# Three PSUM banks in a fixed order for the ten projections of an attention step, and a copy of v moved ahead of part of the gate weights' split

## The chip, the cores and the metric

One core of one Trainium2 chip runs the whole program in a single launch. The metric is the device time of a run in microseconds (us). The engines are TensorE (PE in the profile, with its weight loads as PEld), VectorE (DVE), ScalarE (ACT), GpSimd (POOL) and SyncE (SP), whose queue issues the DMAs.

## The reference

A block of linear attention with decay, and after it a dense layer with a mixture of low-rank experts, both with a layer norm in front and a residual. Cut to what matters:

```
q = rope(x @ Wq.T); k = rope(x @ Wk.T); v = x @ Wv.T      # 32 heads of q, 8 of k and v, 128 wide
dt = softplus(x @ Win.T + dt_bias); g = -dt * exp(A_log_bias)
per chunk of 128 tokens, G = cumsum(g):
  y  = (q k^T * exp(G_i - G_j), causal) @ (v dt)  +  (q exp(G)) @ state
  state = state * exp(G_last) + (k exp(G_last - G))^T @ (v dt)
y = y / rms(y) * gnorm_w * silu(x @ Wg.T)
x = x + y @ Wo.T
x = x + dense(norm(x)) + experts(norm(x))
```

x is 4 images of 512 tokens by 512 features, all in fp32. To keep precision, each fp32 product is taken as three products of "high" and "low" parts in the format fp32r: hi x hi, lo x hi and hi x lo. So every weight and every operand is split into a high half (a copy by ScalarE) and a low half (a subtraction by VectorE).

## The kernel before

Three stages follow each other. The first norms and transposes x, makes the tables, and computes the projections of the first step. The second, attention, has 32 steps, n = 0 to 31. A step takes one group g of heads (8 groups: one head of k and v, four of q) and one image b (4), n = 4 g + b. In the text, "the first step of a group" has b = 0 and "the last step" b = 3. The third stage is the output projection, the second norm and the experts.

TensorE's code is written out for all 32 steps. The other engines run group 0, then a hardware loop over groups 1 to 6, then group 7.

In each step TensorE makes ten projections (units 0 to 9): for the step itself the four gates G0 to G3, one for each chunk of 128 tokens, and for the next step K, Q0 to Q3 and V. Each is 12 matmuls of 128x512 (4 pieces of the contraction, 3 products each). The order on TensorE in a step is: scores of chunk 0, K (unit 0), the state's matmul of chunk 0, G0 (1), mix of chunk 0; scores 1, Q0 (2), state 1, G1 (3), mix 1; scores 2, Q1 (4), state 2, G2 (5), mix 2; Q2 (6), scores 3, Q3 (7), G3 (8), transposes of k, V (9), mix 3, transposes of v.

Each projection fills one PSUM bank. Before the change there are two, and unit number modulo 2 says which. So a unit may start when the unit two before it has been read out (`bank_free`): K and the Qs are read by VectorE, which rotates them (`rotate`, L99: three products, L103 to L105, the last of which counts `rope_terms`); the gates by ScalarE (tanh) and VectorE (`make_gate`, L768, which counts `gate_set`); V by ScalarE (`save_v_rows`, L933, tile `v_t`, which counts `v_set`). GpSimd adds the two rope products (`add_rope`, L108, which counts `roped`).

All engines take their instructions in order, so the order written by hand in `step` matters. On ScalarE the end of a step is: tanh of G3, `save_k`, the high half 1 of wg, `q_high` of the next step's chunk 0 (which waits until all five rope sums of the next step are made), `save_v_rows`, the high half 2 of wg, `save_v` (the copy of the transposed v, tile `v_tok`). The halves of wg occur only in the last step of a group. On VectorE the end of the same step is: gate 3, the low half 1 of wg, `q_low` of the next step's chunk 0, the low half 2 of wg. VectorE splits the low halves of the next wq (L747) near the start of a group's last step, ahead of K's rotation, and ScalarE and VectorE those of wkv in between.

SyncE's queue loads, in one order, the rows of g (`g_row`, 256 KB, one load a chunk), of e, stores z, and in a group's first step loads the next wkv (512 KB, at chunk 1) and wq (2 x 512 KB, at chunk 2), in its last step wg (2 x 512 KB). The row load at chunk 3 is that of the next step's chunk 1; GpSimd waits for its landing (`row_landed(n + 1, 1)`) between its adds for Q2 and Q3.

Of the kernel before, what the change touches and what calls it, by code (L numbers as in the profile page):

```python
# [32 lines left out]
B, L, HID = 4, 512, 512  # L33
# [5 lines left out]
NC = L // C  # L39
# [6 lines left out]
UNITS = 10  # L46
ROPED = 1 + HG
# [5 lines left out]
def wait_ge(engine, sem, count):  # L53

    if not isinstance(count, int) or count > 0:
        engine.wait_ge(sem, count)


def part(w_raw, i):

    return w_raw[i][:, :].rearrange("p (k n) -> p k n", k=KT if i == 0 else KT // 2)


def dst(w, i):

    return w[:, :, :] if i == 0 else w[:, (i - 1) * 2:i * 2, :]
# [354 lines left out]
def attention_stage(nc, io, keep):  # L421
    shared, tab, ident, g_dram, e_dram, z_dram = (keep[k] for k in ("shared", "tab", "ident", "g_dram", "e_dram", "z_dram"))
    with ExitStack() as ctx:
# [3 lines left out]
        def pb(name):  # L427
            return ctx.enter_context(nc.psum_tensor(name, [P, HG, P], F32))

        def sem(name):  # L430
            return ctx.enter_context(nc.semaphore(name))

        w_raw, wkv, wq, wg = (keep[k] for k in ("w_raw", "wkv", "wq", "wg"))
# [23 lines left out]

        z_st = sb("z_st", [P, 2, TB, HG, NC // 2, BL])

        p_proj = [pb(f"p_proj{i}") for i in range(2)]  # L460
        p_y = [pb(f"p_y{i}") for i in range(2)]
        p_score, p_cst = (pb(n) for n in ("p_score", "p_cst"))
        p_tok = keep["p_tok"]
# [5 lines left out]
        rope_terms, roped, v_set = keep["rope_terms"], keep["roped"], keep["v_set"]  # L469
# [4 lines left out]
        gate_set, tanh_set, decay_set = sem("gate_set"), sem("tanh_set"), sem("decay_set")  # L474
        k_split, v_split, q_split, g_split = sem("k_split"), sem("v_split"), sem("q_split"), sem("g_split")
        wk_hi, wv_hi, wq_hi, wg_hi = sem("wk_hi"), sem("wv_hi"), sem("wq_hi"), sem("wg_hi")
# [7 lines left out]
        K_UNIT, V_UNIT, Q_UNIT, GATE_UNIT = 0, 9, (2, 4, 6, 7), (1, 3, 5, 8)  # L484
        LAST = B * KVH - 1

        def ahead(n):

            return not (isinstance(n, int) and n == LAST)
# [3 lines left out]
            return UNITS * n + (at if ahead(n) else GATE_UNIT.index(at))  # L493

        def bank(n, b, at):
            return p_proj[(at if ahead(n) else GATE_UNIT.index(at)) % 2]

        def steps(engine, first, step):

# [10 lines left out]
        def has_last(n):  # L510

            return not (isinstance(n, int) and n == 0)
# [4 lines left out]
        def group_ahead(g):  # L517
            return not (isinstance(g, int) and g == KVH - 1)
# [80 lines left out]

        @block.tensor  # L600
        def _(pe):
            def bank_free(n, b, at):

                if not ahead(n):
                    i = GATE_UNIT.index(at)
                    if i >= 2:
                        pe.wait_ge(gate_set, NC * n + i - 1)
                    elif i == 1:
                        pe.wait_ge(v_set, n + 1)
                    else:  # L610
                        pe.wait_ge(gate_set, NC * n)
                elif at == 0:
                    wait_ge(pe, gate_set, NC * n)
                elif at == 1:
                    pe.wait_ge(v_set, n + 1)
                elif at - 2 in GATE_UNIT:
                    pe.wait_ge(gate_set, NC * n + GATE_UNIT.index(at - 2) + 1)
                else:
                    r = 0 if at - 2 == K_UNIT else 1 + Q_UNIT.index(at - 2)
                    pe.wait_ge(rope_terms, ROPED * (n + 1) + r + 1)  # L620

            def gates(g, b, n, c):
                bank_free(n, b, GATE_UNIT[c])
# [112 lines left out]
        def _(dve):  # L736
# [13 lines left out]
            def g_low_weights(g, i):  # L750

                dve.wait_ge(wg_hi, 2 * g - 2 + i)
                dve.tensor_tensor(dst(wg[1], i), part(w_raw, i), dst(wg[0], i).bitcast(F32), ALU.subtract).then_inc(g_split, 1)
# [21 lines left out]
            def make_probs(n, c):  # L775
                m = NC * n + c
                dve.wait_ge(score_done, m + 1)
                dve.wait_ge(decay_set, m + 1)
                dve.tensor_tensor(probs[:, c % 2], p_score[:, :, :], probs[:, c % 2], ALU.mult).then_inc(probs_set, 1)  # L779
# [52 lines left out]
            def opening_lows(n, pieces):  # L832
                if not ahead(n):
                    for k in pieces:
                        opening_low(dve, keep, k)

            def step(g, b, n):
                make_probs(n, 0)
                q_low(n, b, 1)
                if has_last(n):  # L840
                    make_z(n - 1, 3)
                if group_ahead(g) and b == B - 1:
                    q_low_weights(g + 1)
                if has_last(n):
                    turn_z(n - 1, 3)
                opening_lows(n, (0, 1))
                rotate_next(g, b, n, K_UNIT, 0)
                make_state(n, b, 0)
                make_gate(g, b, n, 0)
                if group_ahead(g) and b == B - 2:  # L850
                    kv_low(wk_hi, k_split, g + 1, 0)
                for c in (1, 2):
                    make_probs(n, c)
                    scale_q(g, b, n, c)
                    q_low(n, b, c + 1)
                    make_z(n, c - 1)
                    opening_lows(n, (2 * c, 2 * c + 1))
                    rotate_next(g, b, n, Q_UNIT[c - 1], c)
                    turn_z(n, c - 1)
                    make_state(n, b, c)  # L860
                    make_gate(g, b, n, c)
                    if c == 1 and group_ahead(g) and b == B - 1:
                        kv_low(wv_hi, v_split, g + 1, D)
                rotate_next(g, b, n, Q_UNIT[2], 3)
                make_probs(n, 3)
                scale_q(g, b, n, 3)
                make_z(n, 2)
                opening_lows(n, (6, 7))
                rotate_next(g, b, n, Q_UNIT[3], 4)
                turn_z(n, 2)  # L870
                if ahead(n):
                    k_low(n + 1, b + 1)
                make_gate(g, b, n, 3)
                if group_ahead(g) and b == B - 1:
                    g_low_weights(g + 1, 1)
                if ahead(n):
                    q_low(n + 1, b + 1, 0)
                if group_ahead(g) and b == B - 1:
                    g_low_weights(g + 1, 2)

            steps(dve, first, step)
            make_z(LAST, 3)
            turn_z(LAST, 3)

        @block.scalar
        def _(act):
# [5 lines left out]
            def half_high(w, i, done, loads):  # L892

                act.wait_ge(w_in[i], 16 * loads)
                act.activation(dst(w[0], i), part(w_raw, i), ACT.Copy).then_inc(done, 1)
# [47 lines left out]
            def save_v(n):  # L943
                act.wait_ge(tok_done, 2 * n + 2)
                wait_ge(act, xw_set, 3 * n)
                wait_ge(act, y_done, NC * n)
                act.activation(v_tok[:, :, :], p_tok[:, :, :], ACT.Copy).then_inc(tok_saved, 1)  # L947
# [13 lines left out]
            def step(g, b, n):  # L961
                if has_last(n):
                    squares(n - 1, 3)
                q_high(n, b, 1)
                make_decay(n, b, 1)
                make_tanh(g, b, n, 0)
                if group_ahead(g) and b == B - 2:
                    act.wait_ge(unit_done, unit(n, K_UNIT) + 1)
                    kv_high(wk_hi, g + 1, 0)
                if not ahead(n):  # L970
                    act.wait_ge(keep["gn_in"], 16)
                opening_highs(n, (0, 1))
                for c in (1, 2):
                    squares(n, c - 1)
                    q_high(n, b, c + 1)
                    make_decay(n, b, c + 1)
                    if c == 1 and group_ahead(g) and b == B - 1:
                        kv_high(wv_hi, g + 1, D)
                    make_tanh(g, b, n, c)
                    opening_highs(n, (2 * c, 2 * c + 1))  # L980
                squares(n, 2)
                if ahead(n):
                    k_high(n + 1, b + 1)
                    make_decay(n + 1, b + 1, 0)
                make_tanh(g, b, n, 3)
                if ahead(n):
                    save_k(n + 1)
                    if group_ahead(g) and b == B - 1:
                        half_high(wg, 1, wg_hi, 2 * g + 2)
                    q_high(n + 1, b + 1, 0)  # L990
                    save_v_rows(n, b)
                    if group_ahead(g) and b == B - 1:
                        half_high(wg, 2, wg_hi, 2 * g + 2)
                    save_v(n + 1)
                    if group_ahead(g) and b == B - 2:
                        act.wait_ge(unit_done, unit(n, Q_UNIT[3]) + 1)
                        half_high(wq, 1, wq_hi, 2 * g + 1)
                        half_high(wq, 2, wq_hi, 2 * g + 1)
                opening_highs(n, (6, 7))
# [588 lines left out]
```

## Time and profile before

| | |
|---|---|
| median of 3 runs | 1941.15 us (1938.84 to 1943.4) |
| the profiled execution | 1941.0 us, span 1939.2 us |
| mean granted TensorE clock | 0.983 of full |
| TensorE matmuls busy | 1832.8 us, 95% of the span |
| VectorE | 1270.4 us, 66% |
| ScalarE | 693.4 us, 36% |
| GpSimd | 643.0 us, 33% |
| DMA | 173.54 MB, 89 GB/s over the span |
| attention stage | from about 77 to 1430 us |

The span runs from the first to the last instruction. Busy time is the time in which an engine works on an instruction; idle time is put down to what ended it ("the releaser"). The granted clock is the share of 2.4 GHz that TensorE was allowed: 1.00 is the level of 2.4 GHz, 0.5 that of 1.2 GHz, and a value between them is a mean over a stretch that has both.

### The profile page before, as it was taken

How to read it: one execution, taken by the hardware profiler on the slowest of the kernel's cores; microseconds unless marked ns; L12 is line 12 of the kernel's file. 1: busy time of each engine (PE TensorE's matmuls, PEld its weight loads, DVE VectorE, ACT ScalarE, POOL GpSimd, SP SyncE). 2: the span in 40 equal slices, each digit the busy share in tenths (PEclk: the TensorE clock that was granted, in tenths of full speed). 3: DMA queues.
4: the chain of work that ended last, by engine and by line, in shares of the span. 5: the costliest groups of instructions: out<-in, count | busy, mean ns of one | idle time of the engine just before them, and what ended most of it. 6: DMA issues, size and time to landing. Idle time of an engine off the chain costs nothing. (4 is left out here: it accounts for less than half of the span.)

```text
span 1939.2 us, 27787 instructions
## 1 busy us (share of the span) xinstructions
PE 1832.8 (95%) x8856; PEld 1482.9 (76%) x8856; DVE 1270.4 (66%) x2340; ACT 693.4 (36%) x2186; POOL 643.0 (33%) x741
## 2 busy tenths in 40 slices
PE   6799999999999999999999999999887999999997
PEld 5588777777777777777777778777766888888885
DVE  7777777787777777777777777777764333333332
ACT  4533443343344434334444434343443112112111
POOL 3444444444444444443444444344400010110100
PEclk9899999999999999999999999999988999999998
DMA  4132332223232223323322232322454322323321
GB/s 153 50 99 83 91 93 70 67 98 92 82 90 94 71 66 93 95 83 91 93 63 70 87 104 77 94 64 63 135 174 155 99 83 81 98 81 92 98 76 33
DMA packets 111073, 173.54 MB, mean 89 GB/s; under 512 B 8016, under 2 KB 45904, under 8 KB 110928
## 3 DMA queue, kind: packets, MB, share of 16 engines
q1 hardware_dynamic: 110928, 171.80, 29.6%
q8 instruction: 67, 1.10, 0.2%
q14 instruction: 78, 0.64, 0.1%
HBM read 133.50 MB, written 38.27 MB: 89 GB/s over the span
## 5 line engine op out<-in xcount | busy, mean ns | idle before, releaser
L84 PE MATMUL p_proj<-wg_hi,shared 128*128 128x512 f32 x1024 | 362.8, 435 | 0.0
L84 PE MATMUL p_proj<-shared,wq_hi 128*128 128x512 f32 x992 | 340.5, 405 | 20.3 <-DVE rope_b L105 20.3
L113 POOL TENSOR_TENSOR q<-rope_a,rope_b 128x512 f32<-128x512 f32 x128 | 165.8, 1295 | 348.8 <-DVE rope_b L105 248.8
L84 PEld LDWEIGHTS p_proj<-wg_hi,shared 128*128 128x128 f32 x1024 | 194.2, 190 | 85.5 <-issue 46.5
L911 ACT ACTIVATE tanh<-p_proj 128x512 f32<-128x512 f32 x128 | 76.6, 599 | 488.5 <-PE p_proj L84 488.5
L84 PEld LDWEIGHTS p_proj<-shared,wq_hi 128*128 128x128 f32 x992 | 189.5, 191 | 69.4 <-DVE rope_b L105 25.5
L84 PE MATMUL p_proj<-wg_lo,shared 128*128 128x512 f32 x512 | 203.3, 397 | 0.0
L84 PE MATMUL p_proj<-shared,wq_lo 128*128 128x512 f32 x496 | 198.6, 400 | 0.0
L84 PE MATMUL p_proj<-shared,wkv_hi 128*128 128x512 f32 x496 | 169.4, 402 | 18.3 <-DVE rope_b L105 18.3
L687 PE MATMUL p_y<-v_tok,probs 128*128 128x128 f32 x1024 | 182.1, 275 | 0.0
L904 ACT ACTIVATE probs<-g_row,stab 128x128 f32<-128x128 f32 x512 | 164.6, 406 | 33.2 <-POOL g_row L1018 33.2
L103 DVE TENSOR_TENSOR rope_a<-p_proj,cos 128x512 f32<-128x512 f32 x155 | 105.0, 677 | 103.0 <-PE p_proj L84 103.0
L929 ACT ACTIVATE square<-p_y 128x128 f32<-128x128 f32 x512 | 134.7, 280 | 91.6 <-PE p_y L687 80.3
L821 DVE SCALAR_TENSOR_TENSOR z<-p_y,srstd,gate 128x128 f32<-128x128 f32 x512 | 143.7, 342 | 29.2 <-issue 19.4
L1144 DVE TENSOR_TENSOR wq_lo<-w_raw,wq_hi 128x1024 fp32r<-128x1024 f32 x63 | 77.1, 1224 | 128.8 <-ACT wq_hi L1139 128.8
L779 DVE TENSOR_TENSOR probs<-p_score,probs 128x512 f32<-128x512 f32 x128 | 88.3, 690 | 97.9 <-PE p_score L84 83.7
L687 PEld LDWEIGHTS p_y<-v_tok,probs 128*128 128x128 f32 x1024 | 150.1, 192 | 3.0
L1036 POOL TENSOR_TENSOR srstd<-svar,mhalf 128x4 f32<-128x4 f32 x128 | 147.6, 1153 | 10.0
L686 PE MATMUL p_y<-state,qs 128*128 128x128 f32 x768 | 148.1, 274 | 0.0
L1488 POOL TENSOR_TENSOR var<-mv,eps 128x1 f32<-128x1 f32 x16 | 3.1, 192 | 432.0 <-DVE mv L1407 432.0
L1028 POOL TENSOR_TENSOR xw<-v_tok,stab 128x512 f32<-128x512 f32 x96 | 104.4, 1088 | 104.7 <-ACT v_tok L947 104.7
L686 PEld LDWEIGHTS p_y<-state,qs 128*128 128x128 f32 x768 | 123.5, 191 | 8.8
(181 smaller groups left out, 3711.3 us busy)
## 6 DMA issues: line engine op xcount, KB each, us to landing
g_row<-g_scratch SPq DMA_DIRECT2D x128, 256.0 KB, 6.0
z_scratch<-z_st SPq DMA_DIRECT2D x256, 128.0 KB
w_raw<-z_scratch SPq DMA_DIRECT2D x63, 512.0 KB, 5.9
e_row<-e_scratch SPq DMA_DIRECT2D x96, 256.0 KB, 3.9
w_raw<-in_wq_t SPq DMA_DIRECT2D x16, 512.0 KB, 8.2
w_raw<-in_wg_t SPq DMA_DIRECT2D x16, 512.0 KB, 5.6
w_raw<-in_wo_t SPq DMA_DIRECT2D x11, 512.0 KB, 5.8
w_raw<-in_wkv_t SPq DMA_DIRECT2D x8, 512.0 KB, 5.0
```

What stands on the lines that cost most here:

```text
L84: mm = pe.matmul(out, lhs[a], rhs[e], start=(i == 0 and j == 0), stop=(i == len(pairs) - 1 and j == 2))
L103: dve.tensor_tensor(rope_a[:, s, :], x, keep["cos"][:, :], ALU.mult)
L113: pool.tensor_tensor(out, keep["rope_a"][:, s, :], keep["rope_b"][:, s, :], ALU.add).then_inc(keep["roped"], 1)
L686: pe.matmul(p_y[c % 2][:, h, :], qs[:, h, :], state[:, c % 2, h, :], start=True, stop=False)
L687: mm = pe.matmul(p_y[c % 2][:, h, :], probs[:, c % 2, h, :], v_tok[:, c, :], start=(c == 0), stop=True)
L779: dve.tensor_tensor(probs[:, c % 2], p_score[:, :, :], probs[:, c % 2], ALU.mult).then_inc(probs_set, 1)
L821: zz = dve.scalar_tensor_tensor(z[:, h, :], p_y[c % 2][:, h, :], srstd[:, c, h:h + 1], gate[:, c % 2, h * D:(h + 1) * D], ALU.mult, ALU.mult)
L904: e = act.activation(probs[:, c % 2, h, :], g_row[:, c % 2, h, :], ACT.Exp, bias=stab[:, b % 2, c, T_BIAS, h:h + 1])
L929: s = act.activation(square[:, h, :], p_y[c % 2][:, h, :], ACT.Square, scale=2.0 / float(np.sqrt(D)), accum_out=ssum[:, c, h:h + 1])
L1028: pool.tensor_tensor(xw[:, c % 2], v, w, ALU.mult).then_inc(xw_set, 1)
L1036: pool.tensor_tensor(srstd[:, c, :], svar[:, c, :], mhalf[:, :], ALU.pow).then_inc(srstd_set, 1)
L1144: dve.tensor_tensor(by_half(keep["z_lo"][slot]), raw_z(keep, raw_slot), by_half(keep["z_hi"][slot].bitcast(F32)), ALU.subtract).then_inc(k ...
```

## The change

The attention stage gets a third bank, and a table says which bank a unit takes. Before a unit starts, TensorE waits until the last unit in the same bank has been read out, in the same step or in the step before. The last step of all, which makes only the four gates, has a table of its own. So K follows Q3 of the step before, G0 follows V, Q0 follows G3 of the step before, G1 follows G0, Q1 follows K, G2 follows Q0, Q2 follows G1, Q3 follows Q1, G3 follows G2, and V follows Q2. In a group's last step, ScalarE makes both high halves of wg later (order: `q_high`, `save_v_rows`, half 1, `save_v`, half 2), and VectorE both low halves after `q_low`.

```diff
-        p_proj = [pb(f"p_proj{i}") for i in range(2)]
+        p_proj = [pb(f"p_proj{i}") for i in range(3)]
...
+        BANKS = (0, 1, 2, 1, 0, 2, 1, 0, 2, 1)
+        LAST_BANKS = (0, 1, 2, 0)
...
         def bank(n, b, at):
-            return p_proj[(at if ahead(n) else GATE_UNIT.index(at)) % 2]
+            return p_proj[BANKS[at] if ahead(n) else LAST_BANKS[GATE_UNIT.index(at)]]
...
+            def taken(n, at):
+
+                if at in GATE_UNIT:
+                    wait_ge(pe, gate_set, NC * n + GATE_UNIT.index(at) + 1)
+                elif at == V_UNIT:
+                    pe.wait_ge(v_set, n + 2)
+                else:
+                    r = 0 if at == K_UNIT else 1 + Q_UNIT.index(at)
+                    pe.wait_ge(rope_terms, ROPED * (n + 1) + r + 1)
+
             def bank_free(n, b, at):
 
                 if not ahead(n):
                     i = GATE_UNIT.index(at)
-                    if i >= 2:
-                        pe.wait_ge(gate_set, NC * n + i - 1)
-                    elif i == 1:
-                        pe.wait_ge(v_set, n + 1)
-                    else:
-                        pe.wait_ge(gate_set, NC * n)
-                elif at == 0:
-                    wait_ge(pe, gate_set, NC * n)
-                elif at == 1:
-                    pe.wait_ge(v_set, n + 1)
-                elif at - 2 in GATE_UNIT:
-                    pe.wait_ge(gate_set, NC * n + GATE_UNIT.index(at - 2) + 1)
-                else:
-                    r = 0 if at - 2 == K_UNIT else 1 + Q_UNIT.index(at - 2)
-                    pe.wait_ge(rope_terms, ROPED * (n + 1) + r + 1)
+                    if LAST_BANKS[i] in LAST_BANKS[:i]:
+                        return taken(n, GATE_UNIT[LAST_BANKS.index(LAST_BANKS[i])])
+                    return taken(n - 1, max(u for u in range(UNITS) if BANKS[u] == LAST_BANKS[i]))
+                here = [u for u in range(at) if BANKS[u] == BANKS[at]]
+                if here:
+                    return taken(n, here[-1])
+                if has_last(n):
+                    taken(n - 1, max(u for u in range(UNITS) if BANKS[u] == BANKS[at]))
...
                 make_gate(g, b, n, 3)
-                if group_ahead(g) and b == B - 1:
-                    g_low_weights(g + 1, 1)
                 if ahead(n):
                     q_low(n + 1, b + 1, 0)
                 if group_ahead(g) and b == B - 1:
+                    g_low_weights(g + 1, 1)
                     g_low_weights(g + 1, 2)
...
                     save_k(n + 1)
-                    if group_ahead(g) and b == B - 1:
-                        half_high(wg, 1, wg_hi, 2 * g + 2)
                     q_high(n + 1, b + 1, 0)
                     save_v_rows(n, b)
                     if group_ahead(g) and b == B - 1:
+                        half_high(wg, 1, wg_hi, 2 * g + 2)
+                    save_v(n + 1)
+                    if group_ahead(g) and b == B - 1:
                         half_high(wg, 2, wg_hi, 2 * g + 2)
-                    save_v(n + 1)
```

## Rows read from the trace of the kernel before

**Rows 1.** The page's first part: busy us, share, instructions by engine.

```profile
PE 1832.8 (95%) x8856; PEld 1482.9 (76%) x8856; DVE 1270.4 (66%) x2340; ACT 693.4 (36%) x2186; POOL 643.0 (33%) x741
```

**Rows 2.** TensorE's groups (busy, mean ns, idle before) and one of its waits (us, times, longest).

```profile
L84 PE MATMUL p_proj<-shared,wq_hi 128*128 128x512 f32 x992 | 340.5, 405 | 20.3 <-DVE rope_b L105 20.3
L84 PE MATMUL p_proj<-shared,wkv_hi 128*128 128x512 f32 x496 | 169.4, 402 | 18.3 <-DVE rope_b L105 18.3
...
PE p_tok L655 <- ACT v_t L936: 4.3, 5, 1.5
```

**Rows 3.** Timeline around V of step 13, TensorE and ScalarE: start, us, instruction, [idle before].

```profile
661.44 0.49 PE L648 MATMUL p_tok<-ident,k 128*128 128x128 f32 x3
662.54 0.50 PE L84 MATMUL p_proj<-shared,wkv_hi 128*128 128x512 f32 x1 [0.61 <-DVE rope_b L105]
...
667.22 0.60 PE L655 MATMUL p_tok<-ident,v_t 128*128 128x128 f32 x4
667.58 0.47 PE L84 MATMUL p_score<-q_hi,k_hi 128*128 128x512 f32 x1
...
703.75 0.50 PE L84 MATMUL p_proj<-shared,wkv_hi 128*128 128x512 f32 x1 [0.61 <-DVE rope_b L105]
...
665.64 0.60 ACT L936 ACTIVATE v_t<-p_proj 128x512 f32<-128x512 f32 x1 [1.11 <-PE p_proj L84]
```

**Rows 4.** TensorE's timeline in step 15, a group's last step: scores 0, K, scores 1, Q0.

```profile
708.79 0.47 PE L84 MATMUL p_score<-q_hi,k_hi 128*128 128x512 f32 x1
...
709.57 0.40 PE L84 MATMUL p_proj<-shared,wkv_hi 128*128 128x512 f32 x1
...
712.36 1.02 PE L672 MATMUL p_cst<-xw,k_tok 128*128 128x512 f32 x2
...
716.82 0.47 PE L84 MATMUL p_score<-q_hi,k_hi 128*128 128x512 f32 x1
...
720.12 0.50 PE L84 MATMUL p_proj<-shared,wq_hi 128*128 128x512 f32 x1 [2.36 <-DVE rope_b L105]
...
724.56 1.02 PE L672 MATMUL p_cst<-xw,k_tok 128*128 128x512 f32 x2
```

**Rows 5.** VectorE's timeline in step 15: wq's low halves, K's rotation, state, Q2's rotation.

```profile
715.11 2.35 DVE L747 TENSOR_TENSOR wq_lo<-w_raw,wq_hi 128x1024 fp32r<-128x1024 f32 x2
...
720.10 0.69 DVE L808 COPY state<-p_cst 128x512 f32<-128x512 f32 x1
...
742.03 0.69 DVE L103 TENSOR_TENSOR rope_a<-p_proj,cos 128x512 f32<-128x512 f32 x1 [3.36 <-PE p_proj L84]
```

**Rows 6.** Timeline of step 16, a group's first: SyncE's issue, GpSimd, TensorE; the issues' landing.

```profile
785.91 1.24 SPq L536 DMA_DIRECT2D g_row<-g_scratch  x2
...
794.77 1.26 POOL L113 TENSOR_TENSOR q<-rope_a,rope_b 128x512 f32<-128x512 f32 x1 [7.08 <-DMA g_row<-g_scratch]
...
797.24 0.66 PE L655 MATMUL p_tok<-ident,v_t 128*128 128x128 f32 x4 [1.05 <-ACT v_t L936]
...
DMA to landing us min/median/max: 8.5/8.6/8.7
```

**Rows 7.** ScalarE's wg copies as a group; timeline of step 16, ScalarE's squares, VectorE's probs.

```profile
L895 ACT ACTIVATE wg_hi<-w_raw 128x1024 fp32r<-128x1024 f32 x14 | 14.8, 1059 | 0.0
...
757.24 0.28 ACT L929 ACTIVATE square<-p_y 128x128 f32<-128x128 f32 x1 [2.17 <-issue]
...
756.89 0.69 DVE L779 TENSOR_TENSOR probs<-p_score,probs 128x512 f32<-128x512 f32 x1 [1.85 <-issue]
...
773.10 0.69 DVE L779 TENSOR_TENSOR probs<-p_score,probs 128x512 f32<-128x512 f32 x1 [0.19 <-PE p_score L84]
```

**Rows 8.** Stretches: busy (x) by engine, granted clock, DMA share, GB/s.

```profile
65.00:80.00 15.00, 7.29 (x24) 5.17 (x25) 8.75 (x18) 8.02 (x18) 4.61 (x6) 0.54 0.37 87
212.70:217.10 4.40, 4.34 (x17) 3.23 (x18) 3.37 (x7) 1.81 (x5) 4.17 (x5) 1.00 0.41 133
720.10:724.50 4.40, 4.38 (x12) 3.47 (x13) 4.00 (x9) 1.81 (x5) 4.28 (x5) 0.61 0.40 130
```

## The prediction

> **What bounds the kernel now.** I began at the page's busy times [rows 1]: TensorE is busy for 1832.8 of 1939.2 us and no other engine for more than 66%. Inside the attention stage nothing but TensorE's own stream can set the time, and a change that takes no matmul away can only return idle time of that engine. So the second view was TensorE's idle time by what ended it [rows 2]. The rope products on VectorE end 18.3 us of idle time ahead of V's projections and 20.3 us ahead of Q projections; the copy of v ends 4.3 us ahead of the transposes of v. Listing the waits one by one (TensorE's timeline, in pieces, over the whole stage) gave three kinds: 31 waits ahead of V, one in every step but the last, of 0.52 us in steps 0 to 3 and 28 to 30 and 0.61 us in the other 24; seven ahead of Q0, of 2.34 to 2.36 us, in step 3 of each group but the last; five of 0.69 to 0.92 us ahead of Q0 in the first step of groups 2 to 6. 7 x 2.35 + 3.87 = 20.3, so the list is whole.
>
> **V's wait, and its price.** The middle of a step without loads [rows 3]: three transposes of k start at 661.44, V at 662.54, 1.10 us later. Four transposes of v take 0.36 us from start to the scores' start (667.22 to 667.58), so three should take 0.27: V starts 0.83 us later than it need, not the 0.61 that the idle column shows, because the refill of the pipeline is lost too. (For the 0.52 waits: 0.74.) With two banks V takes the bank of Q3, whose rotation VectorE has just ended. With the new table V takes bank 1, last used by Q2, which VectorE rotates before probs, qs and z of chunk 3 and before Q3, some 5 us earlier. Gone: 24 x 0.83 + 7 x 0.74 = 25.1 us.
>
> Does something else stop TensorE there? Behind V stand the last mix and the transposes of v, which need ScalarE's copy v_t. In this step ScalarE stood idle for 1.11 us until V was done, and v_t ended at 666.24, 0.98 us ahead of the transposes [rows 3]. V comes 0.83 earlier, so the copy still follows V at once (0.28 left), and the transposes have all of their 0.98. In ordinary steps (41.2 us from one V to the next, 662.54 to 703.75) the 0.83 is kept.
>
> **Q0's wait in a group's last step.** VectorE splits the next wq there: 2.35 us put ahead of K's rotation, which is over just before the state copy starts at 720.10 [rows 5]. Q0 stands in K's bank, so it starts at 720.12 where, counted as scores to projection in the same step (708.79 to 709.57, 0.78), it could have started at 716.82 + 0.78 = 717.60: 2.52 us [rows 4]. In the new table Q0 takes bank 2, freed by the previous step's last gate. A projection takes 2.79 (709.57 to 712.36), so the state matmul of chunk 1 is reached at 720.39; it needs the state that VectorE copies until 720.79, behind the same rotation. About 0.44 of the wait moves there, 2.08 is returned. VectorE then has no pause until it waits 3.36 us for Q2 [rows 5], more than the 2.08, so it has the slack. 7 x 2.08 = 14.6 us. The five waits in first steps give 3.87 + 5 x 0.17 = 4.7 (again the refill; the state copy is early enough by 0.2 to 0.5 us).
>
> **Where it is given back.** In a group's first step the weights of wkv and wq are loaded, 1.5 MB in the same queue. The g rows for the next step, issued at 785.91 behind them, let GpSimd go on at 794.77, after 7.08 us of waiting [rows 6]. GpSimd is in order: its add for Q3 stands behind that landing, ScalarE's q_hi behind the add, v_t behind q_hi, and the transposes of v behind v_t: 1.05 us of TensorE idle already in step 16, 0 to 1.47 in the seven first steps, and in the two without a wait (steps 0 and 12) v_t ends less than 0.1 us ahead of them. The issue hangs on the chunk-2 state of that step, so the landing does not move when only V moves: the whole of V's gain comes back as wait. 0.74 in step 0, 0.83 in step 4.
>
> In steps 8, 12, 16, 20 and 24 more comes back. VectorE there trails TensorE: probs of chunk 2 waited only 0.19 us for its scores [rows 7]. Its start is set by the loop's turn: the squares waited 2.17 us and probs 1.85 us on "issue" [rows 7], released by no semaphore. The change moves one wg_hi copy (1.06 us [rows 7]) behind v_tok, last before that turn. With v_tok 0.83 us earlier, the squares come 0.12 us later than now if the turn counts from the last copy's end; if the turn is hidden behind that copy, the low half of wg on VectorE, which now also ends later, still leaves K's rotation only 0.30 us earlier. I take the middle, 0.09 earlier, and with the 0.17 us of idle the whole chain to the landing moves 0.26 (0.05 to 0.47) instead of the 0.83 + 0.94 + 0.83 that TensorE has gained since the previous V: 2.34 us come back as wait, 11.7 in all. Given back: 0.7 + 0.8 + 11.7 = 13.3 us.
>
> The Trainium skill, "Runtime: NRT & Kernel Launch", section "Instruction fetch mechanics", says that a taken branch to a target that is not in the fetch window stalls until it is fetched. The two idle times on "issue" agree that the loop's turn stalls; whether a running copy hides it no row shows. By the rule, counted from the branch, it would be the 0.30 end, and the sum 1 us larger.
>
> **The moved operations otherwise.** The v_t copy now passes one wg_hi copy, but ScalarE was waiting for GpSimd there anyway (q_hi came late, v_t later still), so this buys nothing. The second low half on VectorE is needed only in the middle of G0 of the next step, at about 758.8 in the frame of step 16 against 756.5 when it is ready: 2.3 us of cover. No DMA moves in its queue; the wait of the loads of wg and wq on the splits is long met. One more bank costs nothing. The last step's gates wait for gates and rotations that are over.
>
> **The clock.** Of the seven long waits, the last four are followed by half clock: the granted clock reads 1.00 in the 4.4 us after the wait in groups 0 to 2 (212.7 is the first) and 0.61 in groups 3 to 6 (720.1 is the first) [rows 8], and Q0 takes 4.44 us instead of 2.82 [rows 4]: 1.6 us each, 6.4 in all. They go with the waits. But the wait ahead of v's transposes grows to about 2.5 to 4 us in five steps, as long as those or longer. At four in seven, five of them cost 5 x 4/7 x 1.6 = 4.6. Net +1.8.
>
> **The sum.** 25.1 + 14.6 + 4.7 = 44.4 returned, 13.3 given back, +1.8 of clock: 32.9 us. The profiled execution took 1941.0 us, of which 1939.2 are the span; the median shown is 1941.15, the same within 0.01%. 1941.0 - 32.9 = 1908.1: **1908 us**. Own range: the clock's part lies between +6.4 and -1.6, the loop's turn within 1 us, and a step's 0.98 us of slack may be shaved once g rows in last steps are the later ones: 1900 to 1915.
>
> **Rivals.**
> - *The landing moves too.* If the g rows arrive earlier than their issue suggests (it takes 8.6 us in first steps under the weight loads, so it may be the transfer that is slow and not the issue that is late), the 13.3 us are kept and no new half clock comes: 44.4 + 6.4 = 50.8, 1890 us. Against it: the queue is in order and the loads stand ahead. 0.12.
> - *The chain Q3, GpSimd, ScalarE, v_t sets every step.* If it is longer than I read by more than 0.28 + 0.98 = 1.26 us, V's gain comes back in ordinary steps too. Left: 14.6 and part of the clock, 1920 to 1928, say 1925. Against it are the 1.11 us of idle time in [rows 3]. 0.12.
> - *No change.* TensorE's wait was a mere label and the start of V or Q0 is set by something else, or VectorE's delay catches TensorE later in the same step: 1941. Against it: rope_b's end and V's start differ by 0.06 us or so at each of the waits I read. 0.05.
> - *Slower: the clock.* As the stage opens, after waits of 6.2, 1.6 and 2.5 us, TensorE works at half clock for about 14 us (0.54 over 65 to 80 us) [rows 8]. If each of the seven first steps' new waits did that, 7 x 7 = 49 us would be lost against 31.1 + 6.4 gained: 1953. It decides from a low stretch of 2 x 37.5/7 = 10.7 us per group. Against it: after 2.36 us the low stretch lasted about 3.4 us (1.6 lost). 0.03. The Trainium skill, "TensorE: Matmul & The Clock Gate", section "HAM oscillation", says that gaps in TensorE's work bring half clock for what follows each of them; the trace agrees in four cases of seven, and that page's rule speaks for this rival.
>
> **How the numbers follow.** My forecast has 0.68. The range 1896 to 1926 takes in my own range and the second rival, and leaves out the first, the third and the fourth (0.20). A change under 0.2% (3.9 us) is no change for this kernel. Faster 0.91, same 0.05, slower 0.04.
>
> **What would show it.** Right: no TensorE idle on rope_b; V follows k's transposes within 0.3 us; ordinary steps of 40.4 us; idle ahead of v's transposes grown from 4.3 to about 18 us, all in first steps, 2.5 to 4 us each from step 8 on; a new wait of 0.4 us on the state copy in last steps; a group of four steps from 170.2 to about 166.2 us plus half clock. Wrong: v's transposes wait in ordinary steps (second rival); their wait stays near 4 us (first rival); the mean granted clock falls below 0.983; VectorE has no idle time left ahead of Q2.

## The result, and the profile after

Four runs of the changed kernel took 1907.9 us (median; 1901.77 to 1910.72), beside 1942.27 us for the kernel before on the same chip: a ratio of 0.9822, 95% interval [0.9807, 0.9836]. Forecast were 1908 us, with a range of 1896 to 1926. The profiled execution took 1906.53 us, of which 1904.7 are the span, so 34.5 us less than the one of before; predicted were 32.9. Line numbers of the attention stage are four to seven higher than before.

The page's busy times, then three of its groups (busy, mean ns, idle before), for the changed kernel; they answer to [rows 1, 2]:

```profile
PE 1824.3 (96%) x8856; PEld 1481.1 (78%) x8856; DVE 1272.7 (67%) x2340; ACT 692.1 (36%) x2186; POOL 645.5 (34%) x741
...
L84 PE MATMUL p_proj<-shared,wq_hi 128*128 128x512 f32 x992 | 335.3, 399 | 0.0
...
L84 PE MATMUL p_proj<-shared,wkv_hi 128*128 128x512 f32 x496 | 171.4, 407 | 0.0
...
L935 ACT ACTIVATE square<-p_y 128x128 f32<-128x128 f32 x512 | 134.2, 279 | 85.7 <-PE p_y L694 80.4 <-issue 5.3
```

TensorE's waits of the same execution (us in total, times, longest):

```profile
PE p_tok L662 <- ACT v_t L942: 14.6, 9, 2.3
...
PE p_cst L679 <- DVE state L815: 5.3, 8, 3.3
```

All 38.6 us of idle time on `rope_b` are gone. What has come in their place is idle time ahead of v's transposes, grown from 4.3 to 14.6 us, and seven waits of 0.3 us on the state copy (the eighth, 3.3 us, is in step 31, stood there before too, and was not part of the sum).

TensorE's timeline of the changed kernel. First V in step 16, 0.25 us behind the transposes of k, then the state's matmul in step 15, then v's transposes in first steps 4 to 24 and in last step 19:

```profile
772.82 0.49 PE L655 MATMUL p_tok<-ident,k 128*128 128x128 f32 x3
773.07 0.48 PE L84 MATMUL p_proj<-shared,wkv_hi 128*128 128x512 f32 x1
...
708.71 1.10 PE L679 MATMUL p_cst<-xw,k_tok 128*128 128x512 f32 x2 [0.30 <-DVE state L815]
...
282.36 0.66 PE L662 MATMUL p_tok<-ident,v_t 128*128 128x128 f32 x4 [1.66 <-ACT v_t L942]
447.12 0.83 PE L662 MATMUL p_tok<-ident,v_t 128*128 128x128 f32 x4 [2.13 <-ACT v_t L942]
613.92 0.66 PE L662 MATMUL p_tok<-ident,v_t 128*128 128x128 f32 x4 [2.30 <-ACT v_t L942]
779.79 0.66 PE L662 MATMUL p_tok<-ident,v_t 128*128 128x128 f32 x4 [1.90 <-ACT v_t L942]
902.88 0.66 PE L662 MATMUL p_tok<-ident,v_t 128*128 128x128 f32 x4 [1.26 <-ACT v_t L942]
945.80 1.12 PE L662 MATMUL p_tok<-ident,v_t 128*128 128x128 f32 x4 [2.16 <-ACT v_t L942]
1112.32 0.66 PE L662 MATMUL p_tok<-ident,v_t 128*128 128x128 f32 x4 [2.27 <-ACT v_t L942]
```

The 4.4 us behind three of these waits (stretch, TensorE's busy time, granted clock, DMA share, GB/s). The stretch behind the 1.90 us stays at 2.4 GHz; 0.61 is a mean over a stretch that is mostly at 1.2 GHz:

```profile
447.10:451.50 4.40, 4.38 (x14) 0.61 0.00 0
613.90:618.30 4.40, 4.38 (x15) 0.61 0.00 0
779.80:784.20 4.40, 4.40 (x20) 1.00 0.00 0
```

**Where the time came from.** The start of k's transposes gives the length of each step. An interval runs from k's transposes near the end of one step to those of the next, so the V that it holds, and the wait of v's transposes, belong to the step before the one that fills most of it. The differences of the two profiled executions, with the prediction's terms sorted the same way:

| intervals from one step's k transposes to the next | before, us | after, us | saved | predicted |
|---|---|---|---|---|
| 7 over a group's last step (Q0's wait, V's wait, old half clock) | 313.0 | 286.6 | 26.4 | 26.7 |
| 7 ordinary | 288.4 | 282.4 | 6.1 | 5.7 |
| the last 3 (steps 28 to 30) | 123.5 | 121.1 | 2.4 | 2.3 |
| 5 pairs around the first steps 8, 12, 16, 20, 24 | 421.8 | 425.1 | -3.4 | -3.3 |
| the pair around step 4 | 83.37 | 82.79 | 0.58 | 0.74 |
| the first two (V of step 0, and its return as wait) | 80.12 | 79.85 | 0.27 | 0 |
| all of the span that lies outside (V of step 30) | 629.0 | 626.9 | 2.1 | 0.7 |

Intervals over last steps fell from between 43.8 and 45.4 us to 40.94 each, ordinary ones from 41.2 to 40.34. What the last row has above V's 0.7 us is at the end of the attention stage, where TensorE was at 1.2 GHz for 6.8 us from 1400 us on in the kernel before, and for 3.4 us near the same place after.

### The profile page after: what moved, and what is told of

It reads as the page before. It is cut to its first block and busy times, and to the rows that moved or that the text cites. A ratio compares the mean times of both kernels' runs of the same rounds, so it can differ in the third digit from the quotient of the medians.

```text
span 1904.7 us, 27787 instructions
## 1 busy us (share of the span) xinstructions
PE 1824.3 (96%) x8856; PEld 1481.1 (78%) x8856; DVE 1272.7 (67%) x2340; ACT 692.1 (36%) x2186; POOL 645.5 (34%) x741
## 5 line engine op out<-in xcount | busy, mean ns | idle before, releaser
L84 PE MATMUL p_proj<-shared,wq_hi 128*128 128x512 f32 x992 | 335.3, 399 | 0.0
L808 DVE TENSOR_TENSOR q_lo<-q,q_hi 128x512 fp32r<-128x512 f32 x128 | 91.6, 716 | 67.3 <-ACT q_hi L924 67.3
```

The lines of the kernel that those rows point to most:

```text
L84: mm = pe.matmul(out, lhs[a], rhs[e], start=(i == 0 and j == 0), stop=(i == len(pairs) - 1 and j == 2))
L808: dve.tensor_tensor(q_part[1][:, :, :], q[b % 2][:, :, c * C:(c + 1) * C], q_part[0][:, :, :].bitcast(F32), ALU.subtract).then_inc(q_lo_se ...
```

## The experiments

Letters stand for the kernels. Each ratio is against the kernel before, run beside it on the same chip. A, B, D and F shared a chip, C, E, G and H a second, I to L a third; times from different chips are compared by these ratios too.

**A. The change again.** No edit.

> The change itself, unaltered, as the neighbour of the other runs on this chip. Both theories: 1902 to 1911 us, 0.979 to 0.985 of before.

1907.7 us, ratio 0.9825 [0.9808, 0.9843]. The profiled execution is the slowest of its five, 1912.08 us, with 18.6 us ahead of v's transposes, where the first profile had 14.6. How long these waits are differs between executions of one kernel.

**B. The banks alone.** ScalarE and VectorE keep the old order of the wg halves.

```diff
+                if group_ahead(g) and b == B - 1:
+                    g_low_weights(g + 1, 1)
                 if ahead(n):
                     q_low(n + 1, b + 1, 0)
                 if group_ahead(g) and b == B - 1:
-                    g_low_weights(g + 1, 1)
                     g_low_weights(g + 1, 2)
```

and the same on ScalarE: both `half_high(wg, ...)` ahead of `save_v`, the first ahead of `q_high`.

> Three banks, with the old order of the gate weights' halves on ScalarE and VectorE. My theory: the banks make the whole gain, and the moved halves only delay VectorE's restart of the loop (its last low half ends about 1.4 us later in the frame of step 16), so K's rotation and, behind it, the g rows' issue in the five first steps inside the loop come up to 1.3 us earlier here: 0 to 6 us faster than the change, about 1904. Rival: the copy of v's rows ahead of the high half is worth something once V comes earlier (v_t would stand behind a copy of 1.06 us in seven steps): up to 7 us slower than the change, and the transposes of v then wait for v_t in every last step of a group.

1903.99 us, ratio 0.9811 [0.9785, 0.9838]. The banks carry the whole gain.

**C. The order alone.** The new order with the two old banks.

> Two banks as before, only the order of wg's halves on ScalarE and VectorE as in the change. My theory: nothing waits for the copy of v earlier, but VectorE's last low half ends later ahead of the loop's turn and K's rotation comes up to 1.3 us later in five first steps, where Q0 waits for it with two banks: 0 to 7 us slower than before, 1941 to 1948. Rival: the order is worth something by itself: faster than 1938.

1946.48 us, ratio 1.0025 [1.0013, 1.0037]: slower by a quarter of a per cent. Ahead of projections (first row), and Q0 in step 16 (second), with Q0's five waits in first steps now 1.10 to 1.89 us where the kernel before had 0.69 to 0.92:

```profile
PE p_proj L84 <- DVE rope_b L105: 42.6, 43, 2.4
...
766.16 0.50 PE L84 MATMUL p_proj<-shared,wq_hi 128*128 128x512 f32 x1 [1.88 <-DVE rope_b L105]
```

Both low halves of wg now stand behind `q_low` on VectorE, and wait there for ScalarE's high halves, so K's rotation comes later: in the mean of first steps 8 to 24 it starts 14.6 us after the k transposes of the step before, against 13.8 us in the kernel before. With two banks Q0 waits for just that rotation. With three it does not.

**D. wq's loads behind the rows, in the changed kernel.** The prediction put all that is given back on the g rows' landing behind wq's 1 MB. This moves the loads past the row load of chunk 3 and takes nothing out.

```diff
-                        if b == 0 and c == 2:
+                        if b == 0 and c == 3:
```

> The change, and in a group's first step the loads of wq are issued after the load of the g rows for the next step, not ahead of it. My theory: the transposes of v wait in first steps (12.9 of 14.6 us) because the g rows stand behind 1 MB of weights. They then land some 3 us earlier, those waits fall below 2 us in all, the four half clock stretches behind them go: 13 + 6 = 19 us faster than the change, about 1889. Rival: the wait is set by VectorE, which trails in these steps, or by the rows' late issue, not by the loads: waits of 10 us or more stay and the time stays above 1902.

1887.65 us, ratio 0.9726 [0.9708, 0.9744], 20 us below the change. SyncE's queue and GpSimd in step 16, first the changed kernel, then D:

```profile
767.89 0.98 SPq L534 DMA_DIRECT2D w_raw<-in_wq_t  x2
769.05 1.11 SPq L540 DMA_DIRECT2D g_row<-g_scratch  x2
...
777.33 1.26 POOL L113 TENSOR_TENSOR q<-rope_a,rope_b 128x512 f32<-128x512 f32 x1 [7.04 <-DMA g_row<-g_scratch]
```

```profile
758.02 0.39 SPq L540 DMA_DIRECT2D g_row<-g_scratch  x1
758.68 0.96 SPq L534 DMA_DIRECT2D w_raw<-in_wq_t  x2
759.93 0.34 SPq L540 DMA_DIRECT2D g_row<-g_scratch  x1
...
764.76 1.78 POOL L113 TENSOR_TENSOR q<-rope_a,rope_b 128x512 f32<-128x512 f32 x1 [4.27 <-DMA g_row<-g_scratch]
```

The rows that Q3's add waits for are issued ahead of the loads and are there 6.7 us later (758.02 to 764.76), against 8.3 us behind them (769.05 to 777.33). In the mean of first steps 8 to 24 they are issued 1.4 us earlier after the k transposes of the step before (36.0 against 37.5 us) and take 1.1 us less to land (7.1 against 8.2 us). v's transposes wait three times, 1.22 us at most, and no first step has half clock behind it.

**E. The same move in the kernel before.**

> The kernel before, and in first steps the loads of wq behind the g rows. My theory: it takes away only the 4.3 us of waits ahead of v's transposes, 1937; the 19 us that the same edit gave on top of the change are there only because the change moves TensorE ahead of the landing. Rival: the landing costs as much with two banks: 1922 to 1928.

1936.35 us, ratio 0.9973 [0.9961, 0.9984]. Its waits on `rope_b` stay whole:

```profile
PE p_proj L84 <- DVE rope_b L105: 38.6, 43, 2.4
```

So the same edit is worth 5 us to the kernel before and 20 us to the changed one. The difference, 15 us, is what the landing took back of the change's gain, half clock behind the waits included.

**F. V again behind Q3.** V's term alone is taken out.

```diff
-        BANKS = (0, 1, 2, 1, 0, 2, 1, 0, 2, 1)
+        BANKS = (0, 1, 2, 1, 0, 2, 1, 0, 2, 0)
```

> The change with one entry of the table altered: V takes bank 0, so it waits for Q3's rotation again (and K for the copy of V). Measures V's term alone. My theory: 0.83 us comes back in 19 of the 31 steps, 16 us slower than the change, less what shorter waits of v's transposes save of half clock (0 to 6): 1917 to 1924. Rival (V's label was empty): within 3 us of the change.

1919.9 us, ratio 0.9891 [0.9871, 0.9911]. V's 31 waits are back in their old size, and v's transposes wait less:

```profile
PE p_proj L84 <- DVE rope_b L105: 18.8, 31, 1.0
...
PE p_tok L662 <- ACT v_t L942: 8.7, 6, 3.0
```

V's part of the change is worth 12 us net, of 25.1 expected back from the waits alone.

**G. Q0 again behind K.** Q0's two terms are taken out, V's stays.

```diff
-        BANKS = (0, 1, 2, 1, 0, 2, 1, 0, 2, 1)
+        BANKS = (0, 1, 0, 1, 2, 0, 1, 2, 0, 1)
```

> The change with a table in which Q0 takes K's bank (0, 1, 0, 1, 2, 0, 1, 2, 0, 1), so it waits for K's rotation and nothing else gets tighter. Measures Q0's term alone. My theory: the seven waits of 2.35 us are back (14.6 us net) and half clock with some of them (0 to 7 x 1.6), the five of first steps cost nothing because they only shorten the wait of v's transposes, which saves half clock there (up to 6): 1918 to 1930, most likely 1924. Rival: Q0's wait only hid VectorE's delay and TensorE meets it later in the step: within 3 us of the change.

1930.22 us (1925.83 to 1934.8), ratio 0.9941 [0.9916, 0.9965], at the top of what was expected. Q0 in two last steps, 3 and 15, and in two first steps, 16 and 20, then the sum:

```profile
210.53 0.50 PE L84 MATMUL p_proj<-shared,wq_hi 128*128 128x512 f32 x1 [2.34 <-DVE rope_b L105]
...
713.00 0.80 PE L84 MATMUL p_proj<-shared,wq_hi 128*128 128x512 f32 x1 [2.33 <-DVE rope_b L105]
756.21 0.50 PE L84 MATMUL p_proj<-shared,wq_hi 128*128 128x512 f32 x1 [1.16 <-DVE rope_b L105]
...
923.45 0.50 PE L84 MATMUL p_proj<-shared,wq_hi 128*128 128x512 f32 x1 [1.88 <-DVE rope_b L105]
...
PE p_proj L84 <- DVE rope_b L105: 23.5, 12, 2.3
```

As in C, Q0's waits in first steps are longer than in the kernel before, by the new order. Q0's part is worth 22.5 us (1930.2 less 1907.7, and the same by the two ratios), with the new order in place; the profiled execution of G has seven stretches at 1.2 GHz in the stage, where the change had four.

**H. B and D together.** The banks alone, with wq's loads behind the rows.

> Three banks, the old order of wg's halves, and the loads of wq behind the g rows. My theory: with no wait left that hangs on VectorE's restart, the old order is worth nothing more: within 2 us of the change with the loads moved, 1885 to 1888. Rival: the old order's 4 us are kept, about 1883, or v_t stands behind the first high half in last steps and it is 3 us slower, 1891.

1889.63 us, ratio 0.9728 [0.9706, 0.9749], no different from D (0.9726), though 1.6 us above what was expected. It has 4.2 us of idle time ahead of v's transposes, in last steps. In two of them (steps 3 and 7) the old order on VectorE meets GpSimd's add for Q3, which takes 2.3 us there. First H in step 7 (VectorE, GpSimd), then the changed kernel in the same step:

```profile
400.72 1.22 DVE L760 TENSOR_TENSOR wg_lo<-w_raw,wg_hi 128x1024 fp32r<-128x1024 f32 x1
...
400.73 2.33 POOL L113 TENSOR_TENSOR q<-rope_a,rope_b 128x512 f32<-128x512 f32 x1 [5.43 <-DMA g_row<-g_scratch]
```

```profile
401.80 1.27 POOL L113 TENSOR_TENSOR q<-rope_a,rope_b 128x512 f32<-128x512 f32 x1 [5.19 <-DMA g_row<-g_scratch]
```

**I. VectorE's new order, ScalarE's old one, with D's edit.**

```diff
                     save_k(n + 1)
+                    if group_ahead(g) and b == B - 1:
+                        half_high(wg, 1, wg_hi, 2 * g + 2)
                     q_high(n + 1, b + 1, 0)
                     save_v_rows(n, b)
                     if group_ahead(g) and b == B - 1:
-                        half_high(wg, 1, wg_hi, 2 * g + 2)
-                    save_v(n + 1)
-                    if group_ahead(g) and b == B - 1:
                         half_high(wg, 2, wg_hi, 2 * g + 2)
+                    save_v(n + 1)
```

> ScalarE splits both halves of the gate weights' high part ahead of v_tok, as in the kernel before; VectorE keeps the new order (one low half, then the probabilities, then the other low half), and wq's loads are issued after the rows. Theory: in last steps GpSimd's add for Q3 is stretched by VectorE's two-input work beside it (1.63 us in the change, 2.33 us with the banks alone), and with the new order on VectorE alone it stays at 1.6 us or below, so the order of ScalarE is worth nothing: 1887 us, within 3 us of the changed kernel with wq after the rows (1887.65). Rival: the copy of v needs its early place on ScalarE, since v_tok starts 1 us later behind the second high half and v's transposes wait for it: 1892 us or above, with v's transposes idle in the last steps by 1 us or more each.

1886.34 us (1885.57 to 1887.23), ratio 0.9718 [0.9697, 0.9739]. Ahead of v's transposes 0.5 us are left in the whole kernel:

```profile
PE p_tok L662 <- ACT v_t L942: 0.5, 2, 0.3
```

The early copy of v is worth nothing here. GpSimd's longest add for Q3 in a last step is 1.77 us, not "1.6 or below", so that part of the expectation was off.

**J. The same without D's edit.**

> The changed kernel with ScalarE's order put back to both high halves ahead of v_tok, VectorE's new order kept, wq's loads where they are. Theory: the waits of v's transposes in the first steps stay at 1.7 to 2.3 us each from step 4 on, and those of the last steps go away or stay under 0.5 us: 1904 us, inside 1899 to 1908. Rival, ScalarE's early copy carries part of the gain: 1910 us or above, with waits of 1 us and more at v's transposes in the last steps.

1899.62 us (1897.12 to 1906.87), ratio 0.9797 [0.9773, 0.9822]; the last steps' waits did not go away (0.97 us in step 3, 1.05 in step 19), and those of first steps from step 4 on were 0.83 to 2.36 us, where 1.7 to 2.3 each was expected; 12.1 us in all.

**K and L. The banks alone, and the change, on the chip of I and J.**

> The banks alone once more, beside the whole change on the same chip. If the copy's new place is worth nothing, the ratio is 0.981 again and no more than 0.1% from the change's. If it is worth what the stretched add on GpSimd costs (0.7 us in each of seven last steps, 5 us), it comes 3 to 5 us above the change, a ratio near 0.985. If it costs, as the first call's 1904 against 1907.7 suggests, it comes 3 to 4 us below.

> The changed kernel as it is, for the comparison on the same chip with the three others: 1908 us, a ratio of 0.982, as in both calls before.

K: 1902.61 us, ratio 0.9808 [0.9782, 0.9834]. L: 1905.5 us, ratio 0.9835 [0.9808, 0.9862]. The change's median lies 3.7 us above that of the banks alone in the first pair and 2.9 us above in the second, with intervals that overlap both times. So the new order bought nothing, and may cost some 4 us. J, which has only VectorE's half of it, lies 5.9 us below L; their intervals overlap a little.

The traces show how ScalarE's half can cost. VectorE's low halves need ScalarE's high halves of the same weights. In the changed kernel ScalarE makes them late and VectorE waits for each; in J it waits for neither. Step 15, first the changed kernel, then J:

```profile
738.13 1.23 DVE L760 TENSOR_TENSOR wg_lo<-w_raw,wg_hi 128x1024 fp32r<-128x1024 f32 x1 [0.74 <-ACT wg_hi L901]
739.57 1.77 DVE L760 TENSOR_TENSOR wg_lo<-w_raw,wg_hi 128x1024 fp32r<-128x1024 f32 x1 [0.21 <-ACT wg_hi L901]
```

```profile
735.27 2.35 DVE L760 TENSOR_TENSOR wg_lo<-w_raw,wg_hi 128x1024 fp32r<-128x1024 f32 x2
```

In the mean of first steps 8 to 24, counted from the k transposes of the step before, K's rotation then starts at 14.6, 14.3 and 14.0 us in the three profiles of the change, at 13.6 and 13.3 with the banks alone and at 13.2 in J; the g rows are issued at 37.5, 37.5 and 37.2, at 37.1 and 36.9, and at 36.4 us. The order of these kernels is that of their times. That the whole 5.9 us come from there is not shown, and in D against I (1887.65, 1886.34), with the first steps' waits gone, there is no difference.

## Why the prediction was right

**What bounds the kernel, and V's wait.** Held. No idle time on `rope_b` is left, V follows k's transposes in 0.25 us, and an ordinary step takes 40.34 us where 40.4 was written: 0.87 us less each, 0.83 predicted. V's price had to be read from start to start; the idle column alone (0.61) adds up to 18.3 us over the stage, almost 7 too few. The copy v_t did keep its slack in ordinary steps: v's transposes wait in none of them, which ends the rival of the chain through Q3, GpSimd and ScalarE. In last steps that chain does come through at times (0.44 us in step 11, 1.26 in step 19, 1.9 us over four of them), which the prediction had only as a remark in its range.

**Q0's wait.** Held: 26.4 us over the last steps against 26.7 (14.6 of Q0, 5.7 of V, 6.4 of half clock). The wait that moves to the state copy is 0.28 to 0.30 us, not 0.44. G gives the same part the other way round. It costs 22.5 us to take back Q0's part, against 14.6 + 4.7 returned and up to 6.4 of clock. C and G also show a cover that the prediction did not price: the new order makes Q0's waits in first steps 0.2 to 1.2 us longer, and only the third bank hides that.

**Where it is given back.** The mechanism is right, by D and E: with the rows ahead of wq's loads the change keeps 15 us more than the kernel before gains by the same edit. The mis-sized term is the 2.34 us that come back in each of five first steps. Measured from k's transposes of the step before, GpSimd goes on after the landing 45.8 us later in the mean of the five, against 46.4 before: the chain moved 0.58 us, where 0.26 was chosen and 0.47 was the upper bound. The issue is not what moved (37.5 against 37.4 us); the landing came 0.7 us sooner after it. "The landing does not move" was taken from the issue alone. Without half clock the five pairs saved 3.0 us (6.4 less 3.4), not 1.3. In steps 0 and 4 together 0.1 us more was kept than predicted.

The sign written down for this part came out only in kind. Idle time ahead of v's transposes was to be about 18 us, all in first steps, 2.5 to 4 us each from step 8 on. It was 14.6 us, 1.9 to 2.3 us in each of those five steps, and 1.9 us of it stood in last steps. Counted from V's start to that of v's transposes, the five first steps lost 7.4 us more than before and the last steps ahead of them 2.6 us, together 10.0 where 11.7 was forecast. A wait in a last step takes away some of TensorE's lead over the next landing, so by this count it mostly stands in for a part of the wait that follows. That may be why the early copy of v has so little to win; no run shows it by itself.

**The loop's turn.** Settled for ScalarE, wrong for VectorE. The changed kernel around it:

```profile
738.00 0.58 ACT L953 ACTIVATE v_tok<-p_tok 128x512 f32<-128x512 f32 x1
738.48 1.06 ACT L901 ACTIVATE wg_hi<-w_raw 128x1024 fp32r<-128x1024 f32 x1
740.57 0.28 ACT L935 ACTIVATE square<-p_y 128x128 f32<-128x128 f32 x1 [1.03 <-issue]
```

From v_tok's start to the squares it is 2.57 us with a copy of 1.06 us between, and 2.78 us without it before (754.46 to 757.24, with the 2.17 us of [rows 7]). So the turn runs while the copy does. The idle time on issue ahead of the squares is 5.3 us in all. The Trainium skill, "Runtime: NRT & Kernel Launch", section "Instruction fetch mechanics", says that a taken branch to a target outside the fetched window stalls until it is fetched. The idle times on issue agree with that; that the stall runs under a copy still at work is what these rows show, and the section does not say it.

On VectorE the prediction had K's rotation 0.09 us earlier (0.30 with the turn hidden). It starts 0.8 us later in the mean of the five first steps (14.6 against 13.8 us), and 0.2 and 0.5 us later in the two other profiles of the change: the prediction let the last low half end later, but by too little, since both low halves wait for ScalarE's high halves and the second takes 1.77 us, where the first takes 1.23. The rows' issue was no earlier either. That the landing still moved is owed to the time from issue to landing (8.2 against 8.9 us in the mean), which the prediction held fixed. Over the three profiles of the change the landing comes 0.6, 0.1 and 1.2 us earlier than before, so that the first lies near the 0.26 that was written is luck.

**The clock.** Half right. The old 6.4 us are gone, as forecast. Of new stretches there were four in this execution where 5 x 4/7 = 2.9 were priced: 6.4 us instead of 4.6. The number is not steady: the three profiles of the change have four, four and two such stretches in the stage. L has one wait that went further:

```profile
615.60 1.11 PE L662 MATMUL p_tok<-ident,v_t 128*128 128x128 f32 x4 [3.95 <-ACT v_t L942]
...
615.60:620.00 4.40, 4.40 (x13) 0.50 0.00 0
```

and the interval with it is 47.3 us long, against 42.4 in K. Executions of L at a mean granted clock of 0.985 took 1903.2 to 1905.8 us, those at 0.981 took 1915.0 and 1915.7. I, without a long wait, has 0.986 to 0.987 in all five, within 1.7 us. The slower rival (every new wait like the opening of the stage) is out.

**The sum.** 32.9 predicted, 34.5 measured. The errors are +1.7 (landing), -1.8 (new half clock), -0.3 (last steps), +0.4 (V elsewhere), +0.1 (steps 0 and 4) and +1.4 at the end of the stage, which was not priced. The two large ones cancel, so the hit is closer than the reasoning deserves.

**The copy's move.** "This buys nothing" held for ScalarE, and the price in VectorE's waits was missed (K and L above). For VectorE's half a benefit was missed. GpSimd's add for Q3 takes 1.27 us alone and 2.33 us when a low half of wg starts 0.01 us ahead of it (H above), and the new order keeps them apart; the longest such add in a last step is 1.72 us in the first profile of the change. The Trainium skill, "SBUF — State Buffer", section "Who interferes with whom", says that a VectorE instruction with two inputs in SBUF contends with a GpSimd instruction that reads SBUF, for ports that one of them holds alone. The trace agrees, since 1.22 + 1.27 = 2.49 is near the 2.33. What it is worth stays under what these runs separate (H 1889.6, D 1887.65, I 1886.3).

## What to carry to other kernels

Price a removed wait from start to start of the instructions around it, not by its idle time, and take the parts out one by one: here they were worth 12 and 22.5 us. A gain on the bounding engine ends at the next thing that does not move with it; here that was a row load of 256 KB behind 1 MB of weights in an in-order queue, and one changed condition, D's, was worth 20 us on top. Look for such a load before looking for more banks. A stage with waits of about 2 us scatters by the clock; with them removed the time is lower and steadier.

## What was unexpected of the hardware

In the fourteen profiles together, in steps 0 to 30, TensorE waited 1.9 us or longer 48 times. Behind 33 of these waits came a stretch at 1.2 GHz, behind 15 none; the shortest with one was 1.97 us and the longest without one 2.91 us. One more stretch stood behind a wait of 1.88 us (G, step 20), and none elsewhere in these steps. In this range the clock does not follow from the wait's length alone. The Trainium skill, "TensorE: Matmul & The Clock Gate", section "HAM oscillation", speaks of longer gaps; the three waits here of 3.5 to 4.0 us agree with it, each with a stretch behind it, and the other 45, all below 3.0 us, are not its case.

One load of g rows of 256 KB took 8.3 us from its issue to the add that waited for it when it stood behind 1 MB of weights in the queue, and 6.7 us when the weights came right after it (step 16; 8.3 and 7.2 us in the mean of five first steps). In D it is also issued 1.2 us sooner behind the stores of z.
